# A field-interaction tower on one core: block 0 in two halves, and the gathers of the first blocks spread anew

## What is computed

```python
x0 = xk = e
for W, b in ((w0, b0), (w1, b1), (w2, b2)):
    z = relu(einsum('bhd,bkd,hks->bsd', x0, xk, W) + b)   # 128 outputs s
    xk, direct = z[:, :64], z[:, 64:]                     # the last layer: all 128 direct
logit = sum over d of the direct parts                    # 256 per sample
h = concatenate([logit, dense_ctx], axis=1)               # 272
y = relu(relu(h @ W_top1 + b_top1) @ W_top2 + b_top2) @ W_top3
```

## Time and profile before

| what | value |
|---|---|
| median of 3 runs | 1256.96 us |
| profiled execution | 1257.96 us |
| its span on the core | 1256.2 us |
| TensorE matmul busy | 1189.4 us, 95% |
| VectorE busy | 1051.0 us, 84% |
| GpSimd busy | 1014.4 us, 81% |
| ScalarE busy | 577.8 us, 46% |
| DMA | 196 MB, mean 156 GB/s |

### The profile page before, as it was taken

How to read it: one execution, slowest core, us unless ns; L and a number is a source line. 1 busy time by engine, 2 the same in 40 slices (tenths; PEclk the granted TensorE clock), 3 DMA queues, 4 the chain that set the end, 5 groups by cost and what they waited for, 6 DMA issues and landing times.

```text
span 1256.2 us, 14871 instructions
## 1 busy us (share of the span) xinstructions
PE 1189.4 (95%) x3864; PEld 726.8 (58%) x3864; DVE 1051.0 (84%) x915; ACT 577.8 (46%) x560; POOL 1014.4 (81%) x637
## 2 busy tenths in 40 slices
PE   0389999999999999999999999999999999999899
PEld 0155656656565666656566665656566665656555
DVE  2278998989899898989899898989988898989761
ACT  1145454544445444454545444444544445454443
POOL 6778898988889898988889898888889888666561
PEclk9989999999999999999999999999999999999999
DMA  4785726264563726356471636456372735643000
GB/s 124 246 263 183 228 64 217 103 216 163 170 209 103 221 77 225 134 174 205 148 226 57 214 115 211 168 170 209 101 216 79 230 135 173 206 141 114 0 1 1
DMA packets 110141, 196.01 MB, mean 156 GB/s; under 512 B 52911, under 2 KB 64270, under 8 KB 110121
## 3 DMA queue, kind: packets, MB, share of 16 engines
q1 hardware_dynamic: 99881, 193.13, 46.5%
q0 software_dynamic: 10240, 2.64, 1.9%
HBM read 193.17 MB, written 12.78 MB: 164 GB/s over the span
## 4 chain that ended last, share of the span: by engine, by line
PE 66%; POOL 17%; issue 8%; DVE 5%; ACT 2%; DMA 1%; DVEq 0%; SPq 0%; POOLq 0%; ACTq 0%
PE acc L813 63%; POOL lo L455 9%; POOL emb L445 8%; DVE prod L711 3%; ACT hi L576 2%; DVE lo L724 1%; DVE acc L711 1%; DVE hi L721 1%; DMA x_tiles<-x_rows 0%; POOL pairs_r L470 0%; DMA x_rows<-x_rows 0%; PE xk L864 0%; PE acc L864 0%; PE acc L891 0%; ACT xk L542 0%
## 5 line engine op out<-in xcount | busy, mean ns | idle before, releaser
L711 DVE TENSOR_TENSOR prod<-x_tiles,xk 128x1024 f32<-128x1024 f32 (+2 forms) x643 | 757.5, 1215 | 139.8 <-PE acc L813 93.6
L455 POOL TENSOR_TENSOR lo<-prod,hi 128x1024 fp32r<-128x1024 f32 (+1 forms) x288 | 688.0, 2391 | 141.5 <-ACT hi L576 136.8
L813 PE MATMUL acc<-prod,wfull 128*128 128x512 f32 (+2 forms) x1408 | 661.1, 594 | 0.0
L576 ACT ACTIVATE hi<-prod 128x1024 fp32r<-128x1024 f32 (+1 forms) x291 | 308.2, 1060 | 406.1 <-DVE prod L711 322.6
L813 PE MATMUL acc<-hi,whi 128*128 128x512 f32 (+1 forms) x800 | 353.4, 442 | 61.3 <-ACT hi L576 61.3
L813 PEld LDWEIGHTS acc<-prod,wfull 128*128 128x128 f32 (+2 forms) x1408 | 266.8, 190 | 206.3 <-issue 177.9
L445 POOL DMA_INDIRECT emb<-table,block_idx x320 | 308.8, 965 | 69.3 <-issue 62.8
L813 PE MATMUL acc<-lo,whi 128*128 128x512 f32 (+1 forms) x736 | 315.4, 516 | 3.2 <-POOL lo L455 2.3
L813 PE MATMUL acc<-hi,wlo 128*128 128x512 f32 (+1 forms) x800 | 316.2, 395 | 0.0
L813 PEld LDWEIGHTS acc<-hi,whi 128*128 128x128 f32 (+1 forms) x800 | 151.1, 189 | 116.4 <-issue 76.5
L813 PEld LDWEIGHTS acc<-lo,whi 128*128 128x128 f32 (+1 forms) x736 | 138.1, 189 | 134.6 <-issue 104.0
(11 more groups left out here) (66 smaller groups left out, 170.9 us busy)
## 6 DMA issues: line engine op xcount, KB each, us to landing
x_tiles<-x_rows SPq DMA_DIRECT2D x304, 512.0 KB, 5.1
x_rows<-x_rows SPq DMA_DIRECT2D x16, 624.0 KB
x_tiles<-x_rows SPq DMA_DIRECT2D x32, 256.0 KB, 5.5
x_stack<-x_rows SPq DMA_DIRECT2D x48, 156.0 KB
emb<-table,block_idx POOLq DMA_INDIRECT x320, 3.7
x_rows<-emb SPq DMA_DIRECT2D x16, 152.0 KB, 3.3
x_tiles<-w SPq DMA_DIRECT2D x1, 768.0 KB, 5.2
x_tiles<-w SPq DMA_DIRECT2D x1, 704.0 KB, 8.1
```

Of the source, the lines that this page charges most:

```text
L455: nc.gpsimd.tensor_tensor(lo[0:r, product_slot(j), :], prod[0:r, product_slot(j), :], hi[0:r, part_slot(j), :].bitcast(f32), ALU.subtract) ...
L576: nc.scalar.activation(hi[0:r, part_slot(j), :], held(n, parity, j)[0:r, :], ACT.Copy).then_inc(hi_ready, 1)
L711: nc.vector.tensor_tensor(held(n, parity, j)[0:r, :], in0, in1, ALU.mult).then_inc(product_ready, 1)
L813: mm = nc.tensor.matmul(z[:, c], w[0:r], part[0:r, c], start=first and i == 0, stop=last and i == len(weights) - 1)
```

## The change

Block 0 gets a smaller copy of its rows in HBM, `x0_first`, in two halves of 32 samples. The host reorders block 0's indices so that a gather fetches four fields by 32 samples; gathers 0 to 9 belong to half 0, 10 to 19 to half 1. SP writes, repeats and loads half 0, then half 1, into the halves of the columns of the same tiles. ScalarE loads the stack's halves from its own queue, directly from the written rows. Layer 0 of block 0 runs on each half: products, roundings, subtractions, matmuls into one bank, ReLUs. Products get 8 slots in place of 6. In steady state SP writes block n + 2's rows behind the thirteenth load in place of the tenth, and take_indices stands ahead of a block's first gather. Block 1's gathers are issued 8 between the two halves' subtractions and 12 in layer 1 of step 0; an explicit table `EARLY` spreads those of blocks 2 to 5, and the parameter `spare` is the number of subtractions at a layer's end that get no gather.

```diff
-PRODS, PARTS = 6, 4
+PRODS, PARTS = 8, 4
+HALF = BLOCK // 2
+GROUP = 128 // HALF
+FIRST = PAIRS // 2
...
+    x0_first = nc.dram_tensor("x0_first", [2, SROWS, BANK], f32, kind="Internal").ap()
...
-            write_rows(0, 0)
-            repeat_rows(0)
-            load_stack(0)
-            for tile in range(T1):
-                if tile_slot(0, tile) == SLOTS - STAGED:
+            def write_first(h):
+
+                done = (first_written, rows_written)[h]
+                sp.wait_ge((first_gathered, rows_gathered[0])[h], 16 * FIRST)
...
+            def repeat_first(h):
+
+                sp.wait_ge((first_written, rows_written)[h], 32)
...
+            def load_firsts(h, start, stop):
+
+                for tile in range(start, stop):
+                    load_first(h, tile)
+
+            write_first(0)
+            repeat_first(0)
+            sp.wait_ge(first_repeated, 16)
+            load_firsts(0, 0, T0 + 4)
+            write_first(1)
+            load_firsts(0, T0 + 4, T0 + 8)
+            repeat_first(1)
+            load_firsts(0, T0 + 8, T1)
+            sp.wait_ge(rows_repeated, 16)
+            load_firsts(1, 0, T1)
             write_rows(1, 1)
             repeat_rows(1)
...
-            WRITE_AFTER = 9
+            WRITE_AFTER = REST - 1
...
             take_indices(0, 0, reuse=False)
-            gather(0, 0, PAIRS)
-            take_indices(1, 1, reuse=False)
-            gather(1, 0, 12)
+            gather(0, 0, FIRST, first_gathered)
+            gather(0, FIRST, PAIRS)
...
-            def layer(n, l, m=None, parity=0, gathers=(0, 0)):
+            def layer(n, l, todo, spare):
...
-                between = max(1, len(tiles) - (4 if l == 2 else 0))
+                between = max(1, len(tiles) - spare)
                 for i, t in enumerate(tiles):
                     subtract(n, at + t)
...
-                    if m is not None and i < between:
-                        gather(parity, start + i * (stop - start) // between,
-                               start + (i + 1) * (stop - start) // between)
+                    for m, parity, q in todo[i * len(todo) // between:(i + 1) * len(todo) // between]:
+                        if q == 0:
+                            take_indices(m, parity)
+                        gather(parity, q, q + 1)
+
+            def fields(m, parity, start, stop):
+                return [] if past_end(m, 0) else [(m, parity, q) for q in range(start, stop)]
...
             GATHERS = {1: (0, 8), 0: (8, 12), 2: (12, PAIRS)}
-            layer(PROLOGUE, 0, 1, 1, (12, PAIRS))
-            take_indices(2, 0)
-            layer(0, 1, 2, 0, GATHERS[1])
+
+            EARLY = [((0, 4), (4, 15), (15, PAIRS), (0, 3)), ((3, 7), (7, 17), (17, PAIRS), (0, 5)),
+                     ((5, 9), (9, 19), (19, PAIRS), (0, 7)), ((7, 11), (11, PAIRS), (PAIRS, PAIRS), (0, 8))]
+            subtract_first(0)
+            take_indices(1, 1, reuse=False)
+            gather(1, 0, 8)
+            subtract_first(1)
+            layer(0, 1, fields(1, 1, 8, PAIRS), 4)
+            for n, (of0, of2, rest, of1) in enumerate(EARLY):
+                parity = n % 2
+                layer(n, 0, fields(n + 2, parity, *of0), 0)
+                layer(n, 2, fields(n + 2, parity, *of2), 2)
+                layer(n + 1, 1, fields(n + 2, parity, *rest) + fields(n + 3, 1 - parity, *of1), 3)
...
-            copy_stack(PROLOGUE)
-            round_hi(PROLOGUE, 1, L0, L2)
-            evacuate(0, 0, accumulator(0, 1), T0, reuse=False)
+            load_first_stack(0)
+            copy_first_stack(0)
+            round_first(0)
+            load_first_stack(1)
+            evacuate_first(0, accumulator(0, 1))
+            copy_first_stack(1)
+            round_first(1)
+            evacuate_first(1, accumulator(0, 1))
...
-            tiles(PROLOGUE, 1, L0, L2)
+            first_tiles(0)
+            first_tiles(1)
+
+            dve.wait_ge(first_rest, (REST + 1) * 16)
...
-            contract(PROLOGUE, L0, L2, accumulator(0, 1))
+            contract(PROLOGUE, L0, L2, accumulator(0, 1), h=0)
+            contract(PROLOGUE, L0, L2, accumulator(0, 1), h=1)
```

More of the change, by code:

```diff
@@ L229, in build @@
         rows_gathered = [sem(f"rows_gathered{p}") for p in range(2)]
+        first_gathered = sem("first_gathered")
+        first_written = sem("first_written")
+        first_repeated = sem("first_repeated")
+        first_stack = [sem(f"first_stack{h}") for h in range(2)]
+        first_copied = sem("first_copied")
+        first_loaded = [sem(f"first_loaded{t}") for t in range(T0)]
+        first_rest = sem("first_rest")
+        first_product = sem("first_product")
+        first_hi = sem("first_hi")
+        first_lo = sem("first_lo")
+        first_used = sem("first_used")
         rows_written = sem("rows_written")
@@ new lines, in repeat_first, with load_first @@
+            def repeat_first(h):
+                sp.wait_ge((first_written, rows_written)[h], 32)
+                sp.dma_start(first_rows(h, FIELDS, [[BANK, FIELDS], [FIELDS * BANK, REPEATS - 1], [1, BANK]]),
+                             first_rows(h, 0, [[BANK, FIELDS], [0, REPEATS - 1], [1, BANK]])
+                             ).then_inc((first_repeated, rows_repeated)[h], 16)
+            def load_first(h, tile):
+                slot = tile_slot(0, tile)
+                if slot == SLOTS - STAGED and h == 0:
+                    sp.wait_ge(wlo_ready, 3)
+                done = tile_loaded[slot] if h else first_loaded[tile] if tile < T0 else first_rest
+                for half in range(2 if tile == TWIN else 1):
+                    parts = slice(half * NEXT, (half + 1) * NEXT) if tile == TWIN else slice(0, 128)
+                    sp.dma_start(x0_tiles[parts, slot, half_columns(h)],
+                                 first_rows(h, SHIFT[tile], [[BANK, parts.stop - parts.start], [1, BANK]])
+                                 ).then_inc(done, 16)
@@ L441, in take_indices, with gather @@
                 pool.nop(nofuse=True)
-            def gather(parity, start, stop):
+            def gather(parity, start, stop, done=None):
                 for i in range(start, stop):
@@ L461, in _, with subtract_first @@
             take_indices(0, 0, reuse=False)
-            gather(0, 0, PAIRS)
-            take_indices(1, 1, reuse=False)
-            gather(1, 0, 12)
+            gather(0, 0, FIRST, first_gathered)
+            gather(0, FIRST, PAIRS)
+            def subtract_first(h):
+                for j in range(L0, L2):
+                    if KIND[j] == "G":
+                        r = rows(*ORDER[j])
+                        pool.wait_ge((first_hi, hi_ready)[h], reached(PROLOGUE, j, "DGH"))
+                        nc.gpsimd.tensor_tensor(lo[0:r, product_slot(j), half_columns(h)],
+                                                prod[0:r, product_slot(j), half_columns(h)],
+                                                hi[0:r, part_slot(j), half_columns(h)].bitcast(f32), ALU.subtract
+                                                ).then_inc((first_lo, lo_ready_g)[h], 1)
             def split_top():
@@ L518, in step @@
-                layer(n, 2, m, parity, GATHERS[2])
+                    layer(n, 0, fields(n + 2, parity, *GATHERS[0]), 0)
+                layer(n, 2, fields(n + 2, parity, *GATHERS[2]), 4)
                 if not past_end(n, 1):
[L520 to L525, removed]
+                    layer(n + 1, 1, fields(n + 3, 1 - parity, *GATHERS[1]), 0)
@@ L526, in _ @@
+            with pool.Fori(len(EARLY) // 2, (BLOCKS - 3) // 2) as g:
                 step(2 * g, 0)
@@ L572, in round_hi @@
                         act.wait_ge(product_ready, reached(n, j, "FDGH"))
-                        if not is_step(n, PROLOGUE) or SPLITS[0].index(ORDER[j][1]) >= PARTS:
-                            act.wait_ge(tile_used, reached(n, parts_before(n, j), "FDGH"))
+                        act.wait_ge(tile_used, reached(n, parts_before(n, j), "FDGH"))
                         nc.scalar.activation(hi[0:r, part_slot(j), :], held(n, parity, j)[0:r, :],
@@ L705, in product @@
                 r = rows(l, t)
-                if not is_step(n, PROLOGUE) or j - L0 >= PRODS:
-                    dve.wait_ge(tile_used, reached(n, product_before(n, j), "FDGH"))
+                dve.wait_ge(tile_used, reached(n, product_before(n, j), "FDGH"))
                 tile = x0_tiles[0:r, tile_slot(1 - parity if l == 0 else parity, TILES[l][t]), :]
@@ L778, in sum_direct2, with first_tiles @@
                 sum_over_d(logit2, direct2, BLOCK * n).then_inc(direct2_summed, 1)
-            tiles(PROLOGUE, 1, L0, L2)
+            def first_tiles(h):
+                dve.wait_ge((first_copied, stack_copied)[h], 1)
+                for j in range(L0, L2):
+                    t = ORDER[j][1]
+                    r, slot = rows(0, t), tile_slot(0, TILES[0][t])
+                    dve.wait_ge(tile_loaded[slot] if h else first_loaded[TILES[0][t]], 16)
```

(16 more changed lines are left out.)

82 lines of the change are left out of this document (61 added, 21 removed).

## The result

The changed kernel takes 1285.62 us (median of four, 1285.56 to 1286.9) against 1257.41 for the kernel before: ratio 1.0227, interval 1.0215 to 1.024. It is 28.2 us slower; 21.8 were forecast. The profiled execution took 1285.56 us, its span is 1283.7; span against span the loss is 27.5 us. S is again the start of layer 1 of step 0 on TensorE.

The account below looks back on a forecast made before the run. The prediction took the kernel as bound by TensorE from 102.40 us on, after a serial start. Step 0 with the start +6.65, steps 1 to 4 +13.8, other steps +1.3 gave +21.8 on 1256.96: 1278.7 us, range 1257 to 1286.

Parts of the forecast that it names:

- S: Start of step 0's layer 1 on TensorE: forecast at 63.4, 7.0 us earlier, bounds 60.2 and 65.5.
- likeliest case: Whole kernel: the forecast of a slower kernel, 1275 to 1284 us, given 44%.
- upper bound of 65.5: Prologue: latest S, if half 1's write waits behind SP's loads too.
- the steps after, and the end: Later steps: take_indices behind layer 1's first subtraction costs about 0.15 us in nine steps, +1.3.
- Block 1's late rows: Step 0: last gather starts at S + 23.2, layer 0 at S + 43.25, 106.65 against 102.40, 4.25 us late.
- The price of half the bytes: Prologue: repeating a half's rows takes between 2.4 and 4.75 us, taken as 4.5.
- Steps 1 to 4: Packed gathers in layer 1 and step 1's late rows: 4.7 + 0.4 + 8.7 = +13.8 us.
- The index copy: Layer 1: behind the first subtraction it makes the third ready at 10.35, wanted at 10.23, about 0.15 us a step.
- What was costed at nothing: Steady steps: PRODS = 8 buys nothing, and SP's write behind the thirteenth load costs nothing.
- Rival A: Whole kernel: faster, the gain at S passes to the end, layer 0 of step 0 below 102.4; 1250 us, 14%.
- B: Rival: rows in time but subtractions late, layer 0 of step 0 at S + 38.6; +15.3, 1272 us, 17%.
- C: Rival: only rows late, a subtraction's lateness in steps 2 to 4 is absorbed; +11.5, 1268.5 us, 14%.

Follow-up runs that it names:

- g_late_wait: c_load_order with VectorE's wait for half 0's 13 other tiles moved to the first product that reads one; 1280.04 us.
- c_load_order: The changed kernel with SP loading only layer 0's 7 tiles of each half first, the other 13 of both halves afterwards; 1282.4 us.
- k_packed: h_best with layer 1's eight gathers in steps 1 to 4 behind its first five subtractions (1,2,1,2,2); 1258.16 us.
- d_both: c_load_order with block 1's gathers back ahead of step 0 (15 and 5), steady spread, index copy ahead of layer 1's first subtraction; 1256.41 us.
- b_steady_spread: The changed kernel with block 1's gathers all back ahead of step 0 (15 and 5) and the old even spread from layer 1 on; 1260.5 us.
- l_before_spare3: The kernel before with layer 2's eight gathers behind its first five subtractions and SP's write behind the thirteenth load; 1251.87 us.
- h_best: g_late_wait with even spread, index copy ahead of layer 1 from step 1 on, block 1's gathers 10 between halves, 8 behind, 2 in layer 1; 1251.6 us.

## Why the prediction was right, and where it was off

The forecast was slower, by 21.8 us; it is 28.2. The direction and the chain behind it were right. That the time lies in the range of 1257 to 1286 is luck, by 0.4 us: it lies above the likeliest case (1275 to 1284), in what was given 3%, and S was beyond its own upper bound of 65.5. By the terms of the sum, in the profiled executions (27.5 us by their spans):

| term | forecast | measured |
|---|---|---|
| S, against 70.37 | -7.0 | -2.0 |
| S to layer 0 of step 0, more than 32.03 | +11.2 | +11.4 |
| from there to layer 0 of step 1, more than 71.87 | +7.1 | +7.5 |
| from there to layer 0 of step 4, more than 3 x 71.87 | +9.1 | +8.1 |
| the steps after, and the end | +1.3 | +2.6 |

- **Block 1's late rows** were the main step and right to 0.2 us: three gathers a subtraction, 6.0 us apart, a last gather at S + 23.1, then 15.5 us of transfers, and layer 0 at S + 43.4 (43.25 forecast). This is a chain from S, so layer 0 keeps about the same distance wherever S is (42.3 to 44.1 us in the five runs with this spread): g_late_wait moved S by 6.3, and layer 0 by 5.9. How TensorE spends the span was less right: 5.0 us of waits for GpSimd in place of 6.6, 3.0 for rows in place of 4.7, and a second stretch at the low clock (last section).
- **S was mis-sized by 5.0 us**, four fifths of the whole miss. The forecast took 4.5 us for the half repeat and 4.2 for the first tile, the prices of transfers with little beside them. In the changed kernel they took 7.55 and 7.75 (47.34 to 55.09), as the chain that ended last shows (start and duration: the last gather, half 1's repeat, its first tile):

```profile
31.39 5.42 DMA emb<-table,block_idx
39.79 7.53 DMA x_first<-x_first
47.34 7.66 DMA x_tiles<-x_first
```

  The sum had the number of SP's issues in it but not the bytes behind them. SP issued a half tile every 0.50 us, not 0.76, and was through 3.7 us before the last gather had landed. That gather took 5.4 us and not 2.4, so the write at 36.83 met the forecast's 36.4 only because two errors cancelled. c_load_order, with fewer loads ahead, has 5.06 for the repeat and at most 4.4 for the tile (44.26 to 48.62, where the product waited for the stack). The sum had the stack off the path once it was in ScalarE's queue; there it came last. The bound of 65.5 had one write behind the loads; repeat and tile stand behind loads as well.
- **The price of half the bytes.** A half repeat took 5.06 us in c_load_order, and half 0's in the changed kernel 5.35 (22.20 to 27.55) with no load of SP's ahead of it; a whole one took 4.75. So half the bytes, in rows of 2 KB, saved nothing at all, and both of my bounds (2.4 and 4.75) lie below. The saving of 0.7 us by the fit of the Trainium skill (DMA: Bandwidth & Descriptors, section Anatomy of one DMA), which the page gives for DMAs of GpSimd, would make it 4.0, an estimate; this repeat, issued by SP, does not bear it out. Whether it is the row's size or other traffic was not tried.
- **Steps 1 to 4.** Step 1 was limited by its rows, as foreseen: from the start of its layer 1 to layer 0 are 34.5 us (156.60 to 191.12), 34.55 forecast. A packed layer 1 costs 1.65 us in k_packed and not the 2.1 that the start times give. TensorE's timeline of the changed kernel shows why a late start and the idle time it leaves are two different prices:

```profile
76.77 1.88 PE L950 MATMUL acc<-prod,wfull 128*128 128x512 f32 x4
78.08 1.03 PE L950 MATMUL acc<-lo,whi 128*128 128x512 f32 x2
78.95 0.40 PE L950 MATMUL acc<-hi,whi 128*128 128x512 f32 x1
...
79.88 1.88 PE L950 MATMUL acc<-prod,wfull 128*128 128x512 f32 x4
82.88 0.73 PE L950 MATMUL acc<-lo,whi 128*128 128x512 f32 x2 [1.13 <-POOL lo L520]
83.45 0.40 PE L950 MATMUL acc<-hi,whi 128*128 128x512 f32 x1
```

  In a stream the lo starts 1.31 us behind the four matmuls' start and the next hi 2.18 behind it. With the wait they come 3.00 and 3.57 behind it. So the lo starts 1.69 us late, which costs 1.39, and which shows as 1.13 of idle: a late start costs 0.3 less than it is late, an idle time 0.26 more than it shows. By that a start 2.1 late would cost 1.8; k_packed has 1.65.
- **The index copy** was forecast at 0.15 us a step and costs 0.24; d_both and b_steady_spread show it, by steps of 71.87 against 72.11. TensorE loses it at the end of layer 1 and not at the third subtraction, where the forecast had it: the last lo group there starts 69.7 us behind layer 0 in d_both and in b_steady_spread, and lasts 1.07 us in the one and 1.22 in the other.
- **The wait in layer 2** of the kernel before shows as 0.16 us and was worth 0.40 a step (l_before_spare3); with the 0.26 of the rows above it comes to 0.42.
- **What was costed at nothing** (PRODS, the later write in even steps) is shown to be nothing. Not foreseen was that the later write is needed for the new spread, and worth 13.4 us there. The forecast of "nothing" held only because the change makes both moves together; that was luck, since the text never weighs the one against the other.
- **Rival A** failed where it was said to be decided: layer 0 of step 0 is at 111.8, not below 102.4. A time near its 1250 was reached only by moving the gathers (h_best, 1251.6). **B** did not come about: layer 0 is at S + 43.4, not + 38.6. **C** is excluded by k_packed.

## What to carry to other kernels

An earlier start is worth only what the next block's chain can follow: trace the last work item that the early start leaves behind, and add its whole way to the consumer. Work for an engine that is nearly full belongs in its idle stretches (here 9.5 and 8.6 us of GpSimd ahead of step 0), and in a steady loop its gaps must be matched against each need time, not against the mean load. When transfers are issued early, order them by who wants them first, and look for waits that cover more than their reader needs.

## What the runs showed of the hardware

TensorE's granted clock fell in gaps shorter than the one I had seen. In step 0's layer 1 TensorE stood still for 1.13, 1.27 and 2.61 us within 13 us, and after the third it ran at 0.51, the 1.2 GHz level, for 3.4 us, as the windows show (the third value from the end):

```profile
92.00:95.00 3.00, 0.39 (x2) 0.13 (x2) 0.01 (x1) 0.00 (x0) 2.98 (x3) 0.99 0.08 7
95.00:98.40 3.40, 3.40 (x9) 2.66 (x10) 2.30 (x3) 1.02 (x1) 3.40 (x2) 0.51 0.40 49
98.40:103.00 4.60, 4.60 (x16) 2.81 (x15) 2.31 (x3) 1.06 (x1) 3.45 (x2) 1.00 0.40 141
```

The forecast had no such stretch there. The length of the gap alone does not decide it. In c_load_order the same layer has waits of 2.52, 1.29 and 2.61 us; behind the first the clock stayed at 1.00, behind the third it fell:

```profile
80.10:82.00 1.90, 1.85 (x8) 1.57 (x9) 1.34 (x2) 1.03 (x1) 1.44 (x2) 1.00 0.06 3
93.50:95.00 1.50, 1.50 (x5) 1.13 (x4) 1.50 (x2) 0.56 (x1) 1.50 (x2) 0.50 0.12 18
```

What does decide it was not tried.

SP's issue of a load has no fixed length either. In the changed kernel a half tile was issued every 0.50 us at first (5.53 for 11) and every 0.65 later (7.11 for 11, from 51.99 on); a whole tile of as many rows took 0.76 in the kernel before (14.50 for 19). From 52 on the 16 DMA engines were full (share 1.05), in the first stretch 0.79. Whether this load or something else sets the pace was not tried, so the length of an issue in one stretch is no safe price for another.
